# Row maximum of causal attention scores: one reduce over the row, or one per 512-column chunk and a small one over the partial maxima

## The chip, the cores and the metric

The kernel runs on the 8 cores of one Trainium2 chip. Each core works alone on one of the 8 batch entries, with no traffic between cores. The metric is the device time of the slowest core in microseconds.

## What is computed

One transformer block over x of shape (8, 2048, 1024) in float32. The input is normalised (layer norm without weights), and attention and a mixture of experts both read that normalised input; their outputs are added to x. In the reference, cut:

```python
xn = _layernorm(x, axis=-1)
x = x + attn(xn, Wq, Wk, Wv, Wo) + ffn(xn, Wg, W1, W2, W3)
# attn: 16 heads of 64, rotary on q and k
scores = jnp.einsum('bhqd,bhkd->bhqk', q, k) * scale      # T = 2048
scores = jnp.where(causal[None, None], -jnp.inf, scores)
attn = jax.nn.softmax(scores, axis=-1)
out = jnp.einsum('bhqk,bhkd->bhqd', attn, v) ... @ Wo.T
# ffn: 8 experts of hidden size 2730, all computed, weighted by a gate that keeps the top 2
```

## The kernel before

The program is written out by hand, one long list per engine, in the order in which `em(...)` is called. `em` (Builder.emit) is given what each operation reads and writes, as ranges of tiles. It tracks them in slots: 512 columns of the PSUM tile `pp` (one bank), 8 columns of the small statistics tile `stat`, 128 columns of the rest. For each slot it knows the last writer and the readers since, and makes the new operation wait for them on the semaphores of their engines. The writer of a slot also waits for an earlier writer or reader on its own engine, by that engine's own semaphore; a wait that the engine has already made for a later value is left out. Engines run their lists in order.

The stages, in order of time: layer norm of 16 token blocks with the gate and the projections of head pair 0 in between; attention for 8 head pairs, each followed by the projections (L336, with the rotary arithmetic on VectorE) and the V product (L382) of the next pair; the output projection (L533); then the 8 experts (L601, L611, L646), which make up nearly two thirds of the span; the output is transposed and stored at the end.

Attention (`emit_hp_attn`) goes through 32 units for each head pair: 16 query blocks of 128 rows by two heads. Unit qb has L = (qb + 1) * 128 key columns, so 128 to 2048. A unit consists of:

- score matmuls, one for each chunk of up to 512 key columns (L464), each into a PSUM bank of its own. From qb = 8 on every unit uses the same four banks; below, the two heads have two banks each
- the row maximum, negated, over all L columns, on VectorE (L472), into one column of `stat`
- the causal mask, added to the last 128 columns only (L476). The maximum is taken before it: any upper bound of the row will do
- the exponential on ScalarE (L482), with that maximum as bias, which also sums the row; the probabilities go to SBUF in bf16
- then, for the **previous** unit, `s2_stage`: 4 dummy matmuls (L401, whose results nobody reads); transposes of the probabilities in groups of four into banks 4 and 5 in turn, each a matmul by a diagonal matrix of the reciprocal row sums (L416); for each group a copy to SBUF on VectorE (L425); 2 more dummy matmuls; the AV matmuls (L435), which wait for all copies; for the second head a copy of the result on ScalarE (L446)
- last, the reciprocal of this unit's row sum (L491) and the diagonal matrix from it (L494), on VectorE

On VectorE the order in a unit is thus: maximum, mask add, copies of the previous unit, reciprocal, diagonal. On TensorE: scores, four dummies, transposes, two dummies, AV matmuls, scores of the next unit. The statistics of even and odd units stand 16 columns apart in `stat` (`st0`): column 0 has the maximum, 2 the row sum, 5 its reciprocal. Columns 8 to 15 are not used in attention.

Of the kernel before, what the change touches and what calls it, by code (L numbers as in the profile page):

```python
# [10 lines left out]
AX = mybir.AxisListType  # L11
# [125 lines left out]
def build_nc():  # L137
# [20 lines left out]
    with contextlib.ExitStack() as ctx:  # L158
# [14 lines left out]
        stat = en(nc.sbuf_tensor("stat", [128, 64], F32))  # L173
        pp = en(nc.psum_tensor("pp", [128, 4096], F32))
# [8 lines left out]
        em = B.emit  # L183
# [7 lines left out]
        def pps(lo_hi):  # L191
# [4 lines left out]
           writes=[("i128f", 0, 128)], dma="cI128F")  # L196
        em("sync", lambda e: e.dma_start(trineg[:], trineg_in),
           writes=[("trineg", 0, 128)], dma="cTRI")
        em("sync", lambda e: e.dma_start(wgr[:], wg_r),
           writes=[("wgr", 0, 64)], dma="cWGR")  # L200
        em("gpsimd", lambda e: e.dma_start(csb[:, 0:T], ct_in),
           writes=[("csb", 0, T)], dma="cCT")
        em("gpsimd", lambda e: e.dma_start(csb[:, T:2 * T], st_in),
           writes=[("csb", T, 2 * T)], dma="cST")
        em("gpsimd", lambda e: e.dma_start(i128b[:], i128_in),
           writes=[("i128b", 0, 128)], dma="cI128B")
        em("gpsimd", lambda e: e.dma_start(sel8[:], sel8_in),
           writes=[("sel8", 0, 1024)], dma="cSEL")
# [188 lines left out]
        def emit_hp_attn(hp):  # L397
            vb = VH[hp % 2]
            def emit_dummies(n):
                for _ in range(n):  # L400
                    em("tensor", lambda e: e.matmul(  # L401
                        pp[:, 3584:4096], i128b[:], csb[:, 0:512],
                        start=True, stop=True),
                       reads=[("i128b", 0, 128), ("csb", 0, 512)],
                       writes=[("pp", 3584, 4096)])

            def s2_stage(q, a, py):
                prb = PRB if py == 0 else PRB_B
                L = (q + 1) * 128
                ngrp = (q + 4) // 4  # L410
                emit_dummies(4)
                for g in range(ngrp):
                    bank = 4 + (g % 2)
                    kb0 = g * 4
                    kbn = min(4, q + 1 - kb0)
                    em("tensor", [(lambda bk, jj, kk, pr, pyy: lambda e: e.matmul(  # L416
                        pp[:, BK(bk)[0] + jj * 128:BK(bk)[0] + (jj + 1) * 128],
                        pb[:, pr + kk * 128:pr + (kk + 1) * 128],
                        dgb[:, pyy * 128:(pyy + 1) * 128],
                        start=True, stop=True))(bank, j, kb0 + j, prb, py)  # L420
                        for j in range(kbn)],
                       reads=[("pb", prb + kb0 * 128, prb + (kb0 + kbn) * 128),
                              ("dgb", py * 128, (py + 1) * 128)],
                       writes=[("pp",) + BK(bank)])
                    em("vector", (lambda gg, bk, n: lambda e: e.tensor_copy(  # L425
                        pb[:, ATT + gg * 512:ATT + gg * 512 + n * 128],
                        pp[:, BK(bk)[0]:BK(bk)[0] + n * 128]))(g, bank, kbn),
                       reads=[("pp",) + BK(bank)],
                       writes=[("pb", ATT + kb0 * 128, ATT + (kb0 + kbn) * 128)])
                reg = 3072 + (q % 2) * 128  # L430
                emit_dummies(2)
                fns = []
                for kb in range(q + 1):
                    tp = (0, 64) if a == 1 else None
                    fns.append((lambda ax, kk, rr, fi, la, tpp, vbb: lambda e: e.matmul(  # L435
                        pp[64 * ax:64 * ax + 64, rr:rr + 128],
                        pb[:, vbb + kk * 128 + 64 * ax:vbb + kk * 128 + 64 * ax + 64],
                        pb[:, ATT + kk * 128:ATT + (kk + 1) * 128],
                        start=fi, stop=la, tile_position=tpp))(
                            a, kb, reg, kb == 0, kb == q, tp, vb))  # L440
                em("tensor", fns,
                   reads=[("pb", vb, vb + (q + 1) * 128),
                          ("pb", ATT, ATT + L)],
                   writes=[("pp", reg, reg + 128)])
                if a == 1:
                    em("scalar", (lambda hh, qq, rr: lambda e: e.copy(  # L446
                        pb[:, AO + hh * T + qq * 128:AO + hh * T + (qq + 1) * 128],
                        pp[:, rr:rr + 128]))(hp, q, reg),
                       reads=[("pp", reg, reg + 128)],
                       writes=[("pb", AO + hp * T + q * 128, AO + hp * T + (q + 1) * 128)])  # L450

            prev = None
            for qb in range(NB):
                for a in range(2):
                    u = qb * 2 + a
                    py = u % 2
                    st0 = 16 * py
                    prb = PRB if py == 0 else PRB_B
                    L = (qb + 1) * 128
                    nch = (L + 511) // 512  # L460
                    sb0 = 1024 if (a == 1 and qb < 8) else 0
                    for c in range(nch):
                        w = min(512, L - c * 512)
                        em("tensor", (lambda aa, qq, cc, ww, b0: lambda e: e.matmul(  # L464
                            pp[:, b0 + cc * 512:b0 + cc * 512 + ww],
                            pb[64 * aa:64 * aa + 64, QHS + qq * 128:QHS + (qq + 1) * 128],
                            pb[64 * aa:64 * aa + 64, KHS + cc * 512:KHS + cc * 512 + ww],
                            start=True, stop=True))(a, qb, c, w, sb0),
                           reads=[("pb", QHS + qb * 128, QHS + (qb + 1) * 128),
                                  ("pb", KHS + c * 512, KHS + c * 512 + w)],  # L470
                           writes=[("pp", sb0 + c * 512, sb0 + c * 512 + w)])
                    em("vector", (lambda LL, b0, s0: lambda e: e.reduce_max(  # L472
                        stat[:, s0:s0 + 1], pp[:, b0:b0 + LL], axis=AX.X,
                        negate=True))(L, sb0, st0),
                       reads=[("pp", sb0, sb0 + L)], writes=[("stat", st0, st0 + 1)])
                    em("vector", (lambda qq, b0: lambda e: e.tensor_tensor(  # L476
                        pp[:, b0 + qq * 128:b0 + (qq + 1) * 128],
                        pp[:, b0 + qq * 128:b0 + (qq + 1) * 128],
                        trineg[:], ALU.add))(qb, sb0),
                       reads=[("pp", sb0 + qb * 128, sb0 + (qb + 1) * 128), ("trineg", 0, 128)],  # L480
                       writes=[("pp", sb0 + qb * 128, sb0 + (qb + 1) * 128)])
                    em("scalar", (lambda qq, b0, s0, pr: lambda e: e.activation(  # L482
                        pb[:, pr:pr + (qq + 1) * 128], pp[:, b0:b0 + (qq + 1) * 128], AF.Exp,
                        bias=stat[:, s0:s0 + 1], scale=1.0,
                        accum_out=stat[:, s0 + 2:s0 + 3]))(qb, sb0, st0, prb),
                       reads=[("pp", sb0, sb0 + (qb + 1) * 128), ("stat", st0, st0 + 1)],
                       writes=[("pb", prb, prb + (qb + 1) * 128), ("stat", st0 + 2, st0 + 3)])
                    if prev is not None:
                        s2_stage(*prev)
                    prev = (qb, a, py)  # L490
                    em("vector", (lambda s0: lambda e: e.reciprocal(  # L491
                        stat[:, s0 + 5:s0 + 6], stat[:, s0 + 2:s0 + 3]))(st0),
                       reads=[("stat", st0 + 2, st0 + 3)], writes=[("stat", st0 + 5, st0 + 6)])
                    em("vector", (lambda s0, pyy: lambda e: e.tensor_scalar(  # L494
                        dgb[:, pyy * 128:(pyy + 1) * 128], i128b[:],
                        stat[:, s0 + 5:s0 + 6], None, ALU.mult))(st0, py),
                       reads=[("i128b", 0, 128), ("stat", st0 + 5, st0 + 6)],
                       writes=[("dgb", py * 128, (py + 1) * 128)])
            if prev is not None:
                s2_stage(*prev)  # L500
                prev = None
# [7 lines left out]
        for g in range(4):  # L509
# [4 lines left out]
               reads=[("wgate", g * 32, (g + 1) * 32), ("i128f", 0, 128)],  # L514
               writes=[("pp", 3584, 4096)])
            em("vector", (lambda gg: lambda e: e.tensor_copy(
                wrow[0:8, gg * 512:(gg + 1) * 512], pp[0:8, 3584:4096]))(g),
               reads=[("pp", 3584, 4096)], writes=[("wrow", g * 512, (g + 1) * 512)])
# [8 lines left out]
        for mc in range(KC if DO_ATTN else 0):  # L527
            em("gpsimd", (lambda m: lambda e: e.dma_start(
                pbs(WOB[m % 2], 1024), wo_l[m]))(mc),
               writes=[("pb", WOB[mc % 2], WOB[mc % 2] + 1024)], dma="woS")  # L530
            for t in range(NT):
# [7 lines left out]
                   reads=[("pb", WOB[mc % 2], WOB[mc % 2] + 1024)] +  # L539
# [255 lines left out]
```

## Time and profile before

| | us |
|---|---|
| median of 2 runs | 6209.49 (5854.96 and 6564.01) |
| the profiled execution | 5854.8 |
| its span on the slowest core (core 4) | 5852.4 |
| spans of the eight cores in it | 5830.1 to 5852.4 |
| TensorE busy | 5163.3 (88%) |
| VectorE busy | 2469.5 (42%) |
| ScalarE busy | 901.1 (15%) |

The profile is of one execution, on the slowest core. PE is TensorE's matmuls and PEld its weight loads, DVE is VectorE, ACT is ScalarE. PEclk is the share of TensorE's clock that was granted in a stretch: 1.00 is 2.4 GHz and 0.50 is 1.2 GHz. A number such as L472 is a line of the kernel. In the timeline consecutive instructions of one line are merged, with the stretch that they take together.

### The profile page before, as it was taken

Reading aid. Unit: us, or ns where it says so; the run is one execution under the profiler, and the core shown is the slowest. Engines: PE = TensorE matmul, PEld = TensorE weight load, DVE = VectorE, ACT = ScalarE, POOL = GpSimd, SP = SyncE. Lnnn points to the kernel's source line nnn. Section 1 sums busy time; section 2 is a strip of 40 time slices with the busy share of each in tenths; the row PEclk is TensorE's granted clock in tenths of the full one; section 3 lists DMA queues with packets and bytes.
Section 4 is the critical chain, followed back from the end, with each engine's and each line's share of the span. In section 5 each row is a group of like instructions: output and inputs, shape, how many; then the busy total and the mean of one; then the engine's idle time right before and its main releaser. Section 6 shows DMA issues by size and latency. Waiting matters only on the chain.

```text
span 5852.4 us, 74425 instructions; the slowest of 8 cores (5830.1 to 5852.4 us)
## 1 busy us (share of the span) xinstructions
PE 5163.3 (88%) x25926; PEld 2447.8 (42%) x26416; DVE 2469.5 (42%) x4116; ACT 901.1 (15%) x1537; POOL 281.3 (5%) x536
## 2 busy tenths in 40 slices
PE   3357787787788789999999999999999999999998
PEld 2333343334333334444444444444444444444444
DVE  3336656656655523333333333333333333333333
ACT  2222212222222211101101101011011011010110
POOL 0000000000000000000000000000000000000000
PEclk8569989999899989999999999999999999999999
DMA  2010000000000022222222222222222222222222
GB/s 43 18 24 1 10 10 4 7 10 10 1 10 3 4 31 37 44 33 36 41 38 37 40 40 38 37 36 39 38 38 38 39 36 41 42 38 33 37 42 81
DMA packets 81889, 173.86 MB, mean 30 GB/s; under 512 B 9336, under 2 KB 9592, under 8 KB 81536
## 3 DMA queue, kind: packets, MB, share of 16 engines
q0 software_dynamic: 76496, 152.13, 17.3%
q1 hardware_dynamic: 5040, 16.94, 0.8%
q8 instruction: 232, 3.80, 0.3%
q14 instruction: 121, 0.99, 0.1%
HBM read 312.74 MB, written 8.39 MB: 55 GB/s over the span
## 4 chain that ended last, share of the span: by engine, by line
PE 83%; DVE 8%; issue 5%; ACT 2%; DMA 1%; DVEq 0%; ACTq 0%; SPq 0%; POOLq 0%
PE pp L601 21%; PE pp L611 21%; PE pp L646 21%; PE pp L401 5%; PE pp L336 3%; PE pp L435 3%; DVE poolb L425 3%; PE pp L464 3%; DVE stat L472 3%; PE pp L416 1%; PE pp L533 1%; PE pp L382 1%; PE pp L259 1%; ACT poolb L482 1%; PE pp L246 1%
## 5 line engine op out<-in xcount | busy, mean ns | idle before, releaser
L601 PE MATMUL pp<-xn,poolb 128*128 128x512 bf16 x5520 | 1330.7, 381 | 6.2 <-issue 0.4
L611 PE MATMUL pp<-xn,poolb 128*128 128x512 bf16 x5518 | 1324.4, 380 | 6.0
L646 PE MATMUL pp<-poolb 128*128 128x512 bf16 x5518 | 1212.4, 379 | 6.0
L625 DVE TENSOR_TENSOR arf<-pp,arf 128x512 f32<-128x512 f32 x704 | 486.9, 692 | 1442.6 <-PE pp L611 1442.6
L611 PEld LDWEIGHTS pp<-xn,poolb 128*128 128x128 bf16 x5632 | 552.8, 98 | 670.4 <-issue 10.5
L601 PEld LDWEIGHTS pp<-xn,poolb 128*128 128x128 bf16 x5632 | 552.4, 98 | 671.0 <-issue 12.6
L646 PEld LDWEIGHTS pp<-poolb 128*128 128x128 bf16 x5632 | 551.1, 98 | 663.8
L621 ACT ACTIVATE arf<-pp 128x512 f32<-128x512 f32 x704 | 420.3, 597 | 2619.0 <-PE pp L601 2619.0
L401 PE MATMUL pp<-csb,i128b 128*128 128x512 bf16 x1416 | 555.4, 392 | 187.9 <-PE pp L464 31.0
L656 DVE TENSOR_TENSOR acc<-acc,pp 128x512 f32<-128x512 f32 x512 | 352.0, 688 | 845.7 <-PE pp L646 829.6
L631 DVE TENSOR_TENSOR poolb<-arf 128x512 bf16<-128x512 f32 x704 | 487.7, 693 | 74.8 <-DVE arf L625 2.3
L472 DVE TENSOR_REDUCE stat<-pp 128x1 f32<-128x128 f32 (+15 forms) x256 | 330.5, 1291 | 322.2 <-PE pp L464 322.2
L425 DVE CAST poolb<-pp 128x512 bf16<-128x512 f32 (+3 forms) x640 | 364.0, 606 | 156.9 <-PE pp L416 152.8
L482 ACT ACTIVATE poolb<-pp,stat 128x128 bf16<-128x128 f32 (+15 forms) x256 | 298.7, 1167 | 761.0 <-DVE pp L476 595.5
L401 PEld LDWEIGHTS pp<-csb,i128b 128*128 128x128 bf16 x1536 | 148.6, 97 | 545.3 <-issue 539.8
L416 PE MATMUL pp<-dgb,poolb 128*128 128x128 bf16 x2176 | 205.7, 227 | 118.1 <-DVE poolb L425 112.9
L336 PE MATMUL pp<-xn,poolb 128*128 128x512 bf16 x999 | 225.1, 384 | 2.0 <-issue 0.9
L416 PEld LDWEIGHTS pp<-dgb,poolb 128*128 128x128 bf16 x2176 | 145.9, 100 | 174.5 <-issue 152.9
L435 PE MATMUL pp<-poolb 128*64 128x128 bf16 x2176 | 183.6, 235 | 39.8 <-DVE stat L491 32.7
L246 PE MATMUL pp<-i128f,arf 128*128 128x128 f32 x128 | 31.0, 423 | 206.0 <-DVE arf L242 206.0
L435 PEld LDWEIGHTS pp<-poolb 128*64 128x64 bf16 x2176 | 145.7, 119 | 111.1 <-issue 111.1
L593 POOL DMA_DIRECT2D poolb<-w_l x176 | 93.5, 531 | 1975.3 <-PE pp L601 1975.2
(78 smaller groups left out, 1665.6 us busy)
## 6 DMA issues: line engine op xcount, KB each, us to landing
poolb<-w_l POOLq DMA_DIRECT2D x352, 256.0 KB, 4.8
poolb<-w_l POOLq DMA_DIRECT2D x128, 352.0 KB, 4.4
arf<-x SPq DMA_DIRECT2D x16, 512.0 KB, 3.5
out<-arf SPq DMA_DIRECT2D x16, 512.0 KB, 2.8
poolb<-wq_l POOLq DMA_DIRECT2D x8, 256.0 KB, 3.8
poolb<-wqs_l POOLq DMA_DIRECT2D x8, 256.0 KB, 4.7
poolb<-wk_l POOLq DMA_DIRECT2D x8, 256.0 KB, 5.4
poolb<-wks_l POOLq DMA_DIRECT2D x8, 256.0 KB, 5.0
```

The source lines that it names most:

```text
L336: em("tensor", [(lambda bk, wb, kkc, fi, la, a0, a1: lambda e: e.matmul(pps(BK(bk)), pb[:, wb + kkc * 128:wb + (kkc + 1) * 128], xn[:, kkc ...
L401: em("tensor", lambda e: e.matmul(pp[:, 3584:4096], i128b[:], csb[:, 0:512], start=True, stop=True), reads=[("i128b", 0, 128), ("csb", 0, ...
L416: em("tensor", [(lambda bk, jj, kk, pr, pyy: lambda e: e.matmul(pp[:, BK(bk)[0] + jj * 128:BK(bk)[0] + (jj + 1) * 128], pb[:, pr + kk * 12 ...
L425: em("vector", (lambda gg, bk, n: lambda e: e.tensor_copy(pb[:, ATT + gg * 512:ATT + gg * 512 + n * 128], pp[:, BK(bk)[0]:BK(bk)[0] + n * ...
L435: fns.append((lambda ax, kk, rr, fi, la, tpp, vbb: lambda e: e.matmul(pp[64 * ax:64 * ax + 64, rr:rr + 128], pb[:, vbb + kk * 128 + 64 * a ...
L472: em("vector", (lambda LL, b0, s0: lambda e: e.reduce_max(stat[:, s0:s0 + 1], pp[:, b0:b0 + LL], axis=AX.X, negate=True))(L, sb0, st0), re ...
L601: em("tensor", [(lambda cc, tt, bk, kkc, fi, la: lambda e: e.matmul(pps(BK(bk)), pb[:, W1B[cc % 2] + kkc * 128:W1B[cc % 2] + (kkc + 1) * 128],
L611: em("tensor", [(lambda cc, tt, bk, kkc, fi, la: lambda e: e.matmul(pps(BK(bk)), pb[:, W2B[cc % 2] + kkc * 128:W2B[cc % 2] + (kkc + 1) * 128],
L621: em("scalar", (lambda bk, tbb: lambda e: e.activation(arfs(SIL[tbb], 512), pps(BK(bk)), AF.Silu))(b1, tb), reads=[("pp",) + BK(b1)], writ ...
L625: em("vector", (lambda bk, tbb, ebb, tt: lambda e: e.tensor_tensor(arfs(H2S[tbb], 512), pps(BK(bk)), arfs(WBC[ebb] + tt * 512, 512), ALU.m ...
L631: em("vector", (lambda cll, tt, tbb: lambda e: e.tensor_tensor(pb[:, HIDB + cll * T + tt * 512:HIDB + cll * T + (tt + 1) * 512], arfs(SIL[ ...
L646: em("tensor", [(lambda mm, tt, bk, cll, fi, la: lambda e: e.matmul(pps(BK(bk)), pb[:, W3B[mm % 2] + cll * 128:W3B[mm % 2] + (cll + 1) * 128],
```

## The change

For units with more than one chunk of key columns, the one reduce over the row becomes one reduce for each chunk, issued right behind that chunk's score matmul, into columns 8 to 11 of the unit's statistics, and a last reduce over these partial maxima, negated, into the column where the maximum stood. Units with one chunk (L up to 512) keep the one reduce. All else stays, and the exponential reads the same value.

```diff
@@ -469,10 +469,24 @@
                            writes=[("pp", sb0 + c * 512, sb0 + c * 512 + w)])
-                    em("vector", (lambda LL, b0, s0: lambda e: e.reduce_max(
-                        stat[:, s0:s0 + 1], pp[:, b0:b0 + LL], axis=AX.X,
-                        negate=True))(L, sb0, st0),
-                       reads=[("pp", sb0, sb0 + L)], writes=[("stat", st0, st0 + 1)])
+                        if nch > 1:
+                            em("vector", (lambda cc, ww, b0, s0: lambda e: e.reduce_max(
+                                stat[:, s0 + 8 + cc:s0 + 9 + cc],
+                                pp[:, b0 + cc * 512:b0 + cc * 512 + ww],
+                                axis=AX.X))(c, w, sb0, st0),
+                               reads=[("pp", sb0 + c * 512, sb0 + c * 512 + w)],
+                               writes=[("stat", st0 + 8 + c, st0 + 9 + c)])
+                    if nch > 1:
+                        em("vector", (lambda n, s0: lambda e: e.reduce_max(
+                            stat[:, s0:s0 + 1], stat[:, s0 + 8:s0 + 8 + n], axis=AX.X,
+                            negate=True))(nch, st0),
+                           reads=[("stat", st0 + 8, st0 + 8 + nch)],
+                           writes=[("stat", st0, st0 + 1)])
+                    else:
+                        em("vector", (lambda LL, b0, s0: lambda e: e.reduce_max(
+                            stat[:, s0:s0 + 1], pp[:, b0:b0 + LL], axis=AX.X,
+                            negate=True))(L, sb0, st0),
+                           reads=[("pp", sb0, sb0 + L)], writes=[("stat", st0, st0 + 1)])
```

## Rows read from the trace of the kernel before

**Rows 1.** The page: engine busy (share) xinstructions, and the group of the row maximum.
```profile
PE 5163.3 (88%) x25926; PEld 2447.8 (42%) x26416; DVE 2469.5 (42%) x4116; ACT 901.1 (15%) x1537; POOL 281.3 (5%) x536
...
L472 DVE TENSOR_REDUCE stat<-pp 128x1 f32<-128x128 f32 (+15 forms) x256 | 330.5, 1291 | 322.2 <-PE pp L464 322.2
```

**Rows 2.** Windows, attention of pairs 1 to 7: length, busy (x) of PE, PEld, DVE, ACT, POOL.
```profile
586.00:2010.00 1424.00, 1121.19 (x7329) 550.59 (x7452) 857.33 (x1619) 327.58 (x587) 16.36 (x31) 0.95 0.04 7
```

**Rows 3.** Chain of waits, attention stage (411 to 2010 us), shares by line.
```profile
by line: PE pp L401 19.5%; issue 12.3%; PE pp L336 12.1%; PE pp L435 11.2%; DVE poolb L425 10.7%; PE pp L464 10.6%; DVE stat L472 9.9%; PE pp L416 4.9%; PE pp L382 3.2%; ACT poolb L482 2.5%; DVE pp L476 1.4%; DVE stat L491 1.0%; DVEq L691 0
```

**Rows 4.** Timeline, 2048 unit, full clock: start, length, instruction, count, [idle before <-releaser].
```profile
973.90 1.03 PE L464 MATMUL pp<-poolb 64*128 64x512 bf16 x4
...
975.04 2.29 DVE L472 TENSOR_REDUCE stat<-pp 128x1 f32<-128x2048 f32 x1 [1.78 <-PE pp L464]
...
976.67 0.61 PE L416 MATMUL pp<-dgb,poolb 128*128 128x128 bf16 x8
977.43 0.30 DVE L476 TENSOR_TENSOR pp<-pp,trineg_s 128x128 f32<-128x128 f32 x1
977.64 2.48 DVE L425 CAST poolb<-pp 128x512 bf16<-128x512 f32 x4
...
980.26 1.00 PE L435 MATMUL pp<-poolb 128*64 128x128 bf16 x15
...
981.19 1.03 PE L464 MATMUL pp<-poolb 64*128 64x512 bf16 x4
```

**Rows 5.** Timeline, a unit with one chunk (L = 512), full clock.
```profile
848.19 0.39 PE L464 MATMUL pp<-poolb 64*128 64x512 bf16 x1
...
848.68 0.69 DVE L472 TENSOR_REDUCE stat<-pp 128x1 f32<-128x512 f32 x1 [0.48 <-PE pp L464]
```

**Rows 6.** VectorE groups by shape: count, busy us, mean ns, idle before.
```profile
L476 DVE TENSOR_TENSOR pp<-pp,trineg_s 128x128 f32<-128x128 f32 x256 | 76.8, 300 | 27.7 <-DVE stat L472 1.4
...
L472 DVE TENSOR_REDUCE stat<-pp 128x1 f32<-128x2048 f32 x16 | 36.7, 2292 | 44.7 <-PE pp L464 44.7
...
L472 DVE TENSOR_REDUCE stat<-pp 128x1 f32<-128x512 f32 x16 | 11.1, 692 | 7.7 <-PE pp L464 7.7
...
L291 DVE TENSOR_REDUCE stat<-stat 128x1 f32<-128x8 f32 x16 | 2.6, 161 | 1.6
```

**Rows 7.** Timeline of VectorE in the layer norm: a reduce without a wait.
```profile
366.28 1.23 DVE L271 COPY acc<-pp 128x1024 f32<-128x1024 f32 x1 [5.61 <-PE pp L265]
367.42 0.16 DVE L277 TENSOR_REDUCE stat<-pp 128x1 f32<-128x8 f32 x1
```

**Rows 8.** Timeline of VectorE: mask add and first copy at L = 640, at L = 1536.
```profile
860.84 0.30 DVE L476 TENSOR_TENSOR pp<-pp,trineg_s 128x128 f32<-128x128 f32 x1
...
862.05 0.89 DVE L425 CAST poolb<-pp 128x512 bf16<-128x512 f32 x2 [0.91 <-PE pp L416]
...
925.23 0.30 DVE L476 TENSOR_TENSOR pp<-pp,trineg_s 128x128 f32<-128x128 f32 x1
925.49 1.83 DVE L425 CAST poolb<-pp 128x512 bf16<-128x512 f32 x3
```

**Rows 9.** Timeline, 2048 units of pair 1 at half clock (16 such units).
```profile
772.40 2.29 DVE L472 TENSOR_REDUCE stat<-pp 128x1 f32<-128x2048 f32 x1 [3.62 <-PE pp L464]
...
774.83 1.06 PE L416 MATMUL pp<-dgb,poolb 128*128 128x128 bf16 x8
...
775.57 1.29 DVE L425 CAST poolb<-pp 128x512 bf16<-128x512 f32 x2 [0.47 <-PE pp L416]
...
782.31 2.29 DVE L472 TENSOR_REDUCE stat<-pp 128x1 f32<-128x2048 f32 x1 [3.62 <-PE pp L464]
```

**Rows 10.** Windows of head pair 1 and of head pair 2: columns as before, granted clock sixth.
```profile
611.00:799.00 188.00, 146.75 (x937) 71.80 (x951) 108.63 (x211) 46.84 (x84) 1.05 (x2) 0.86 0.04 6
824.00:999.00 175.00, 130.27 (x942) 65.30 (x956) 108.16 (x211) 46.83 (x84) 1.05 (x2) 0.99 0.04 6
```

**Rows 11.** Cores: span and mean granted clock of TensorE.
```profile
core 4: 5852.4 us, clock 0.955
...
core 6: 5831.4 us, clock 0.962
```

## The forecast of the time

> **What bounds the kernel now.** I read the page first. TensorE (PE) is busy for 88% of the span [rows 1]. The table by stage puts attention of head pairs 1 to 7, with the projections between them, into 1424 us [rows 2]. There PE works for 1121 of 1424 us: here the engines wait for each other. The experts' stage behind it is the bulk of the span and does not hold the changed line. The chain of waits over the attention stage [rows 3] gives the changed instruction, the row maximum of L472, 9.9% of 1599 us, that is 158 us. It is busy for 330 us in all [rows 1], so about half of it is covered. Where, and by what, decides the sum.
>
> So I followed one unit (one query block of one head) in the timeline. [rows 4] is a unit with L = 2048 key columns at full clock. Its four score matmuls (L464) start at 973.90. The reduce starts at 975.04, when the last is done, 1.14 us after the first began, and runs 2.29 us. The mask add (L476) starts at 977.43 and the copies of the previous unit (L425) at 977.64. The AV matmuls (L435) wait for the last copy and start at 980.26, and the next unit's score matmuls at 981.19, a period of 7.29 us. PE had the first two groups of transposes (L416) done at about 977.28 (976.67 + 0.61), 0.36 us before the first copy started. So in this unit VectorE (DVE) sets the pace from 975.04 to the end of the copies, and what delays the mask add delays the unit.
>
> It is not so everywhere. With L = 640 [rows 8] the mask add starts at 860.84 and the copy only at 862.05, 1.21 us later, waiting for PE's transposes behind the dummy matmuls. Where nothing else is waited for, that distance is 0.21 us [rows 4], so 1.00 us is cover. At L = 1536 [rows 8] it is 0.26, a cover of 0.05 us. From 1664 columns on I take none, as in [rows 4].
>
> **The change part by part.** Units with L up to 512 (8 of 32 in each of the 8 head pairs) keep their one reduce. In the others (24 of 32) one reduce becomes nch reduces of up to 512 columns, each behind its own score matmul, and one over the nch results. PE, ScalarE (ACT) and the DMA queues issue what they issued before, and no instruction passes another queue's; only DVE's work changes.
>
> Earlier start. With one chunk the reduce starts 0.49 us after its matmul began (848.68 minus 848.19, [rows 5]); with four, 1.14 us [rows 4]. So each full chunk takes 0.217 us of PE time, and the first partial reduce of a 2048 unit starts 0.65 us earlier than the old one. DVE is free then: it had been idle for 1.78 us before 975.04 [rows 4].
>
> More instructions. A reduce takes 692 ns over 512 columns and 2292 ns over 2048 [rows 6]: 1.042 ns a column and 0.159 us fixed. Four of 512 are 2.768 us, 0.48 more. The reduce over the partials I price by L291, the same operation over 8 columns of the same tile: 161 ns [rows 6].
>
> Waits between them. The partial results are columns of one 8-wide tracking slot of stat. So each partial reduce waits on VectorE's own semaphore for the one before it, and the last for all of them. Trace of before: between the old reduce and the mask add, which has such a wait, DVE idles 27.7 us over 256, 0.108 us [rows 6]; I use 0.105 (977.33 to 977.43). There are nch of these waits: nch - 1 between partials, one before the last reduce. The mask add, on the other hand, loses its wait, since the last reduce already waited for everything that it needs. An unheld small reduce behind a long copy starts 0.09 us before that copy's recorded end (367.42 against 366.28 + 1.23, [rows 7]). I take 0.09 of overlap for the mask add; between 0 and that I can't tell, as no unheld instruction behind a tiny reduce stands in the trace.
>
> The Trainium skill ("VectorE: DVE Perf Modes", section "The DRAIN you can't avoid") states that eight copies cost the same with a semaphore after each as with one at the end. This trace disagrees: 0.108 us of idle time with a wait, 0.09 us of overlap without. By that rule the splits would be nearly free; what that would make of the time is rival A.
>
> Sum for a 2048 unit, mask add after the first matmul's start: 0.49 + 2.768 + 4 x 0.105 + 0.161 - 0.09 = 3.75 us. Before: 3.53 us. Later by 0.22 us. For L = 1920 the earlier start is worth 0.05 us less while the fixed terms stay: 0.27; for 1792, 0.32; for 1664, 0.37. For 1536, three chunks: 2 x (0.159 + 0.105) + 0.161 - 0.09 - 2 x 0.217 = 0.165, of which 0.05 is covered: 0.12. For 1408 it is 0.22 against a cover of about 0.19 (my interpolation between 0.05 at 1536 and 1.00 at 640 is 0.14 for each 128 columns): 0.03. Below that the delay (0.14 to 0.36) lies within the cover: nothing. With two units of each length: 2 x (0.22 + 0.27 + 0.32 + 0.37 + 0.12 + 0.03) = 2.66 us a head pair, 21 us over eight.
>
> What hides it at the low clock. Some late units run at half the clock, period 9.91 us instead of 7.29 (772.40 to 782.31, [rows 9]). There the reduce ends at 774.69 and the mask add starts 0.1 later, but the copy starts at 775.57, when the first transposes are done, which began only at 774.83 because of the dummies. PE bounds such a unit; the partial reduces would start still earlier, and the change costs nothing. On the profiled core 16 of the 64 units of 1664 and more columns are of that kind, as the distances between their mask adds in the timeline show. That takes off 16 x 0.3 = 5 us. Direct cost: **+16 us**.
>
> What is late next. ACT's exponential starts after the mask add, on a path of its own that ends before the copies do in the long units; it moves along with them. PE's queue holds transposes 3 and 4, the AV matmuls and the next scores behind the copies: its quiet stretch, from 977.28 to 980.26 in [rows 4] 3.0 us with 8 transposes and 2 dummies in it, grows by the 0.2 to 0.4 us. The clock fell only in units with 1792 columns and more, where that stretch is longest, and oftenest in the 2048 ones. In [rows 10] the head pair with five units at half clock takes 188 us in the window where one with none takes 175. The eight cores of this one execution differ by 21 us with the granted clock, 0.955 to 0.962 [rows 11]. A stretch 0.3 us longer puts a unit where one with some 256 columns more stood. I estimate about one more unit at half clock in each head pair, at 1.2 to 2.6 us (the low period against the full one, whole or in part): **+12 us**, half of what separates the cores. The lower bound of this term is 0, the upper is rival B.
>
> The Trainium skill ("TensorE: Matmul & The Clock Gate", section "HAM oscillation — how this bites in real kernels") says that a kernel whose matmul groups are parted by long waits falls back to the low clock again and again. It speaks against this change, and the trace agrees as far as the last units of [rows 9] go.
>
> 5855 + 16 + 12 = 5883 us. The profiled execution took 5854.8 us by the clock of the run, 5852.4 its span, and the sum stands against that; the median of the two runs shown (6209.49) lies 6% higher, halfway between 5854.96 and 6564.01, and my number is for an execution like the profiled one and the lower of the two.
>
> **The rivals.**
> A, the split is free or gains. If the waits between dependent reduces cost nothing and they overlap by 0.09 us, the mask add of a 2048 unit comes at 0.49 + 2.768 - 4 x 0.09 + 0.161 - 0.09 = 2.97 us, 0.56 earlier. The copies then wait for PE's transposes and only 0.32 us of it counts (the 0.36 us above less 0.04 to 0.05 from a group's end to its copy); for 1920 about 0.18, for 1792 0.05, less below: 1.1 us a head pair, -9 us, 5846 us. With waits of zero and no overlap the delays are between 0 and 0.05 us: 5855. Against it: [rows 6] show 0.108 us behind exactly this kind of instruction. A variant of it: the delay is real, but PE covers more than I read. Together 5840 to 5862.
>
> B, the low clock takes over (slower than before). If PE's longer quiet stretch brings each head pair to five low units as pair 1 has [rows 10], the cost is 13 us a pair, 104 us, of which the profiled execution already pays about 39 (the 16 units): +65 us, and about 5 to 10 for the delay in the rest: 5925 us. From 2% on (5972 us) about 60 low units at 2.6 us would be needed instead of 16, 7 to 8 in every pair: all from 1664 columns on. For it: the stretch grows in just these units. Against it: pair 2 had not one in this execution [rows 10], and 0.3 us is a tenth of the stretch.
>
> C, DVE pays more than I took. If the mask add does not overlap but waits as before, each unit is 0.2 us later: 2 x 6 x 0.2 x 8 = 19 us more, 5900 us. The two ends of that price (-0.09 and +0.105) bound it.
>
> **How the numbers follow.** The forecast, 5865 to 5905 with C in it, 0.6. A, 0.15. B short of 2%, 5905 to 5970, 0.2; B beyond 2%, 0.04. Something that I don't see, such as fewer falls of the clock by luck, 0.01. The predicted time is the forecast's, 5883. The range takes in A's lower bound and most of B: 5845 to 5930. Differences within 2% (117 us) are about what a measurement of this kernel can't tell from no change: same 0.94; slower 0.05, B in full; faster 0.01, as nothing on the path shortens by so much.
>
> **What would show it.** In the profile after: the partial reduces over 512 columns at 692 ns, with idle time of about 0.105 us between them; the small reduce at about 160 ns; the mask add of a 2048 unit 3.75 us after its first score matmul; a period of 7.5 us at full clock, unchanged for L up to 1280. Right in the total by accident if the periods stay and the clock alone changes. Wrong, if the partial reduces follow without a gap (A), or if the windows of the head pairs all show a clock under 0.9 (B).

## The result, and the profile after

The changed kernel takes 5923.88 us in the median of 11 runs (from 5904.09), the kernel before 5877.14 us in the median of 10 (from 5854.96). The ratio is 1.0088, 95% interval [1.0066, 1.0110]: about 52 us slower, within the 2% band. In some executions of every kernel the four cores of one die show a lower clock and take some per cent longer; the ratios, and the means over cores further down, leave these out, which is why the medians differ by less. The profiled execution took 5902.4 us, 47.6 more than the one profiled before.

The page and the table of cores after: VectorE's reduces are 576 instead of 192 in the units with more than one chunk (beside 192 small ones), and the clock is lower on every core (before: 0.955 to 0.962). TensorE's busy time can't be compared from the two pages: the trace of core 4 lacks 490 matmul records that this one, of core 0, has. On one and the same core it rises by 25 us (core 3) to 61 us (core 1), on core 4 by 37 us (5163.3 to 5200.4).

```profile
PE 5264.9 (89%) x26416; PEld 2466.2 (42%) x26416; DVE 2544.5 (43%) x4692; ACT 901.6 (15%) x1537; POOL 282.4 (5%) x536
...
L473 DVE TENSOR_REDUCE stat<-pp 128x1 f32<-128x512 f32 (+3 forms) x576 | 360.0, 625 | 221.6 <-PE pp L464 181.3
```

```profile
core 0: 5900.0 us, clock 0.946
...
core 5: 5870.8 us, clock 0.955
```

The groups by shape, count, busy us, mean ns, idle before (answering to [rows 6]). The partial reduces cost what a reduce of 512 cost before, the small one 157 ns, and the mask add (L490) has lost its idle time: 7.5 us over 256 where it was 27.7.

```profile
L473 DVE TENSOR_REDUCE stat<-pp 128x1 f32<-128x512 f32 x432 | 298.8, 692 | 206.3 <-PE pp L464 181.3 <-PE pp L416 0.5
L490 DVE TENSOR_TENSOR pp<-pp,trineg_s 128x128 f32<-128x128 f32 x256 | 74.8, 292 | 7.5 <-issue 0.5 <-DVE stat L486 0.5
...
L480 DVE TENSOR_REDUCE stat<-stat 128x1 f32<-128x4 f32 x64 | 10.0, 157 | 7.6 <-DVE stat L473 1.1
```

The timeline of a unit with L = 1920 at full clock, core 0, from its score matmuls to those of the next unit (it answers to [rows 4], with 128 columns less):

```profile
1810.11 0.98 PE L464 MATMUL pp<-poolb 64*128 64x512 bf16 x4
1810.60 2.94 DVE L473 TENSOR_REDUCE stat<-pp 128x1 f32<-128x512 f32 x4 [1.08 <-PE pp L464]
...
1812.83 0.61 PE L416 MATMUL pp<-dgb,poolb 128*128 128x128 bf16 x8
1813.65 0.16 DVE L480 TENSOR_REDUCE stat<-stat 128x1 f32<-128x4 f32 x1
1813.72 0.29 DVE L490 TENSOR_TENSOR pp<-pp,trineg_s 128x128 f32<-128x128 f32 x1
1813.92 2.34 DVE L425 CAST poolb<-pp 128x512 bf16<-128x512 f32 x4
...
1817.28 0.98 PE L464 MATMUL pp<-poolb 64*128 64x512 bf16 x4
```

The first partial reduce starts 0.49 us after the first score matmul, as worked out. Four of them take 2.94 us with three waits of about 0.1 us in between (2.634 for the reduces alone). The mask add comes at 3.61 us; the forecast sum for 1920 columns was 3.62. Before, it came at 3.35. The period is 7.17 us. With 2048 columns the mask add comes at 3.75 us, the forecast's number (median in e5, described below; before 3.54).

From the traces of all eight cores I took the distance from one unit's first score matmul to the next one's, where the clock was full throughout (median; of 1920 and 2048 columns the first or second unit of the two, as given), and the time at half clock between the first score matmul and the start of the last unit:

| | before | after | later | forecast |
|---|---|---|---|---|
| L up to 1280 | 3.33 to 5.40 us | the same | 0.00 | 0 |
| L = 1408 | 5.450 | 5.465 | 0.015 | 0.03 |
| L = 1536 | 5.728 | 5.822 | 0.094 | 0.12 |
| L = 1664 | 6.101 | 6.463 | 0.362 | 0.37 |
| L = 1792 | 6.541 | 6.850 | 0.309 | 0.32 |
| L = 1920, first | 6.917 | 7.173 | 0.256 | 0.27 |
| L = 2048, first | 7.293 | 7.50 (in e5, where the clock stays full; pairs 0, 1, 3) | 0.21 | 0.22 |
| attention, mean of the cores | 1575.7 us | 1623.6 us | 47.9 | 28 |
| of it at half clock | 118 us | 229 us | 111 | |

One thing in these periods was not in the sum. In the second unit with L = 1664 and in the first with 2048, VectorE has in most pairs one gap that is longer than elsewhere, and the period is up to 0.35 us longer for it. It stands at another instruction from pair to pair. On core 7 of e5 a partial or the small reduce waits 0.46 us instead of 0.105, or the mask add or the first copy starts 0.23 or 0.13 us behind the instruction ahead of it instead of 0.08 or 0.09 us before its end; pairs 6 and 7 have none with 1664 columns, pairs 0, 1 and 3 none with 2048. The gaps of 0.46 us stand in the same pair at the same instruction on all eight cores. The second 1664 unit of pair 2 on core 7:

```profile
927.06 2.68 DVE L479 TENSOR_REDUCE stat<-pp 128x1 f32<-128x512 f32 x4 [0.86 <-PE pp L470]
...
930.19 0.16 DVE L486 TENSOR_REDUCE stat<-stat 128x1 f32<-128x4 f32 x1 [0.46 <-DVE stat L479]
```

In two such units, a packet of the instruction queue q14 (8 KB) started within the unit, 3.9 to 4.3 us after its first score matmul and in both 0.6 us behind the end of the gap. Such a packet starts in these two units in all eight pairs of this core, 3.1 to 4.8 us after the first score matmul, also in the pairs without a longer gap. VectorE's list is longer now and q14 carries 131 packets, before 121. That the gap has to do with the fetch of instructions is a guess from this and not shown. At up to 0.35 us, twice a pair, it is at most 6 us.

All of the loss is in attention: what lies outside it takes 4259 to 4269 us a core before and 4259 to 4266 after.

### The profile page after: what moved, and what is told of

It reads as the page before. It is cut to its first block, busy times and chain, and to the rows that moved or that the text cites. A ratio compares the mean times of both kernels' runs of the same rounds, so it can differ in the third digit from the quotient of the medians.

```text
span 5900.0 us, 76259 instructions; the slowest of 8 cores (5870.8 to 5900.0 us)
## 1 busy us (share of the span) xinstructions
PE 5264.9 (89%) x26416; PEld 2466.2 (42%) x26416; DVE 2544.5 (43%) x4692; ACT 901.6 (15%) x1537; POOL 282.4 (5%) x536
## 4 chain that ended last, share of the span: by engine, by line
PE 83%; DVE 9%; issue 5%; ACT 2%; DMA 1%; DVEq 0%; ACTq 0%; SPq 0%; POOLq 0%
PE pp L615 21%; PE pp L625 21%; PE pp L660 20%; PE pp L401 6%; PE pp L336 3%; PE pp L435 3%; DVE poolb L425 3%; DVE stat L473 3%; PE pp L464 2%; PE pp L416 1%; PE pp L547 1%; PE pp L382 1%; PE pp L259 1%; PE pp L246 1%; PE pp L265 0%
## 5 line engine op out<-in xcount | busy, mean ns | idle before, releaser
L401 PE MATMUL pp<-csb,i128b 128*128 128x512 bf16 x1536 | 618.5, 403 | 153.6
L473 DVE TENSOR_REDUCE stat<-pp 128x1 f32<-128x512 f32 (+3 forms) x576 | 360.0, 625 | 221.6 <-PE pp L464 181.3
```

The costliest lines, as they stand in the source:

```text
L401: em("tensor", lambda e: e.matmul(pp[:, 3584:4096], i128b[:], csb[:, 0:512], start=True, stop=True), reads=[("i128b", 0, 128), ("csb", 0, ...
L473: em("vector", (lambda cc, ww, b0, s0: lambda e: e.reduce_max(stat[:, s0 + 8 + cc:s0 + 9 + cc], pp[:, b0 + cc * 512:b0 + cc * 512 + ww], a ...
```

## The experiments

For each run the ratio to the kernel before stands with its 95% interval. "Attention" is the mean over the cores of the profiled execution, "half clock" the part of it at a granted clock of 0.50.

| | ratio | attention, us | half clock, us |
|---|---|---|---|
| before | 1 | 1575.7 | 118 |
| the change | 1.0088 [1.0066, 1.0110] | 1623.6 | 229 |
| e1: before, mask add delayed | 1.0132 [1.0089, 1.0174] | 1639.9 (cores 0 to 3) | 291 (cores 0 to 3) |
| e2: the change for L to 1536 only | 1.0032 [1.0011, 1.0052] | 1601.2 | 196 |
| e8: e2 again | 1.0046 [1.0020, 1.0072] | 1591.4 | 161 |
| e3: partials don't wait for each other | 0.9922 [0.9896, 0.9949] | 1530.8 | 17 |
| e4: before, with dummies | 0.9952 [0.9932, 0.9973] | 1550.0 | 26 |
| e5: the change, with dummies | 0.9994 [0.9978, 1.0010] | 1565.5 | 5 |
| e6: e3 with dummies | 0.9924 [0.9899, 0.9949] | 1528.6 | 8 |
| e7: before, one unit a pair delayed | none (one execution counts) | 1580.4 | 125 |
| e9: before, two units a pair delayed | 1.0008 [0.9935, 1.0081] | 1595.6 | 182 |
| e10: e2 with dummies | 0.9981 [0.9962, 1.0000] | 1563.9 | 63 |

The theory, called D below: the split delays the mask add and the copies behind it; this costs the time directly in the long units, and once more because TensorE's longer quiet stretch makes its clock fall more often. The rival, S: something of the split itself, its many semaphores and small reads of PSUM, disturbs TensorE.

**e1: the delay without the split.** In the kernel before, in units with four chunks, behind the one reduce:

```diff
+                    if nch == 4:
+                        for j in range(2):
+                            em("vector", (lambda jj, s0: lambda e: e.reduce_max(
+                                stat[:, s0 + 8:s0 + 9],
+                                stat[:, s0 + (8 if jj else 0):s0 + (9 if jj else 1)],
+                                axis=AX.X))(j, st0),
+                               reads=[("stat", st0 + (8 if j else 0), st0 + (9 if j else 1))],
+                               writes=[("stat", st0 + 8, st0 + 9)])
```

> The kernel before with its one reduce, and behind it, in the units with four chunks (L from 1664), two tiny reduces on VectorE that depend on each other. They do nothing but delay the mask add: by 2 x (0.105 + 0.161) + 0.071 - 0.266 = 0.34 us a unit, about what the changed kernel does to these units (0.36 to 0.21). Theory D (the delay of the mask add and nothing else of the split costs the time, half of it directly and half through TensorE's clock): direct 8 x 8 x 0.34 = 22 us less what falls in units at half clock, about 18, and 25 to 35 us more by the clock; ratio 1.007 to 1.010, time at half clock per core in attention up from 118 us to over 200. Rival S (the many semaphores or small reads of PSUM of the split themselves disturb PE's clock): 18 to 22 us alone, ratio 1.003 to 1.004, and half-clock time as before.

Measured: ratio 1.0132. The tiny reduces show up as worked out, 154 ns each:

```profile
L479 DVE TENSOR_REDUCE stat<-stat 128x1 f32<-128x1 f32 x128 | 19.7, 154 | 14.0 <-DVE stat L473 0.5 <-DVE stat L479 0.5
```

The full-clock periods are 0.32 to 0.33 us longer in these units (6.43, 6.86, 7.24 us against 6.10, 6.54, 6.92), 21 us over the 64 of them. On cores 0 to 3, the ones that count here, attention takes 62 us more than on the same cores before, and 291 us of it are at half clock instead of 124. No split is needed for either part of the loss: S falls as the explanation of the changed kernel (e3, further down, has the change's partial reduces and next to no half-clock time, which speaks against S too). The ratio is above the 1.007 to 1.010 that theory D gave. The clock's part is larger than I expected, and larger than with the change, whose delay is smaller in just the longest units (0.21 to 0.26 us against 0.32), where the clock falls most. Not all of it lies in the long units: 31 of the 291 us are in the first 24 units of the pairs, where the kernel before has none and e1 delays nothing (more on such falls under e10).

**e2 and e8: the split in the short units alone.** `if nch > 1` became `if 1 < nch < 4` in both places, so that units from L = 1664 keep the one reduce.

> The change in the units with two and three chunks alone (L 640 to 1536); from 1664 on the one reduce stays. Theory D: these units have cover, direct cost 2 x (0.10 + 0.02) x 8 = 2 us, and their clock never falls, so the time is that of before within 3 us, ratio 1.000, and half-clock time about 118 us a core. Rival S: the clock falls here too, +10 us and more.

> The kernel of e2 once more (the split in the units with two and three chunks alone), to see whether its surplus repeats: e2 gave 1.003 and 196 us a core at half clock where e7, with a like delay made otherwise, gave 125. Both theories on e2 expect 1.002 to 1.004; if it was the luck of that chip or hour, 1.000.

Measured: 1.0032 and 1.0046, not 1.000. The periods behave as in the table above (5.822 us at 1536, 6.104 at 1664), the direct cost is the 2 us expected, and still half-clock time goes up to 196 and 161 us. Of these, 35 and 21 us lie in the first 24 units of the pairs, where the kernel before has none, and 86 us in both runs in the last unit and the projections behind it (before 61). The full-clock periods in these two places are those of before, but for the 0.02 to 0.09 us at 1408 and 1536 columns. That was a miss: a surplus of 10 us and more was what rival S expected of e2. e7, e9 and e10 were made for it.

**e3: partial maxima that don't wait for each other.** The changed kernel, with the partial results in slots of their own (in a wider stat), read with a stride by the last reduce:

```diff
-                                stat[:, s0 + 8 + cc:s0 + 9 + cc],
+                                stat[:, 64 + 2 * s0 + 8 * cc:65 + 2 * s0 + 8 * cc],
...
-                            stat[:, s0:s0 + 1], stat[:, s0 + 8:s0 + 8 + n], axis=AX.X,
+                            stat[:, s0:s0 + 1],
+                            stat[:, 64 + 2 * s0:96 + 2 * s0].rearrange(
+                                "p (c w) -> p c w", w=8)[:, 0:n, 0:1], axis=AX.XY,
```

> The changed kernel with each partial maximum in a tracking slot of its own (8 columns apart, read with a stride by the last reduce), so that the partial reduces do not wait for each other. Forecast from the rows: gaps between partials go from +0.105 us to between -0.04 and -0.09; the mask add of a 2048 unit comes 3.16 us after its first score matmul (before 3.53, changed 3.75), where the copies then wait for TensorE's transposes. Periods at full clock against the kernel before: -0.31 (2048), -0.18 (1920), -0.05 (1792), 0 (1664 and below): -9 us in all. With the clock falling less often than before: 10 us more. Theory D: 5830 to 5850 us, ratio 0.995 to 0.999. If the wait on the own semaphore costs nothing beyond what the engine needs anyway: the same as the changed kernel, ratio 1.009.

Measured: ratio 0.9922, 46 us faster than before and faster than the forecast for it. Timeline of a 2048 unit at full clock (core 3):

```profile
955.70 1.03 PE L464 MATMUL pp<-poolb 64*128 64x512 bf16 x4
...
956.19 2.48 DVE L473 TENSOR_REDUCE stat<-pp 128x1 f32<-128x512 f32 x4 [0.80 <-PE pp L464]
...
958.47 0.61 PE L416 MATMUL pp<-dgb,poolb 128*128 128x128 bf16 x8
958.79 0.16 DVE L480 TENSOR_REDUCE stat<-stat 128x1 f32<-128x4 f32 x1
958.86 0.29 DVE L492 TENSOR_TENSOR pp<-pp,trineg_s 128x128 f32<-128x128 f32 x1
959.06 2.61 DVE L425 CAST poolb<-pp 128x512 bf16<-128x512 f32 x4
```

Four partial reduces of 512 columns take 2.48 us in all, less than 4 times 0.692: each starts 0.09 us before the recorded end of the one ahead. In the changed kernel the same four take 3.075 us (2.768 and three gaps; median over its 2048 units). The wait on the engine's own semaphore is worth 0.2 us a time, gap and lost overlap together. The mask add comes 3.16 us after the first score matmul, as forecast. The copies start 0.20 us later, at 3.36 us and not at the 3.43 that I had for the transposes' end: the first copy waits for the first group of four transposes alone (done at about 958.85), not for both groups. So the periods fall by more than worked out: 6.906 us at 2048 (by 0.39), 6.585 at 1920 (0.33), 6.335 at 1792 (0.21), 6.029 at 1664 (0.07), which is 16 us over the eight pairs. The clock gives most of the rest: 17 us at half clock instead of 118, worth 26 us at the price worked out under e5. Together 42 of the 45 us by which attention is shorter.

**e4, e5, e6: keeping the clock up.** Three dummy matmuls before the third group of transposes, in units whose previous query block has 13 or more key blocks; in the kernel before (e4), the changed one (e5) and e3's (e6):

```diff
+                    if g == 2 and q >= 12:
+                        em("tensor", [lambda e: e.matmul(
+                            pp[:, 3584:4096], i128b[:], csb[:, 0:512],
+                            start=True, stop=True)] * 3,
+                           reads=[("i128b", 0, 128), ("csb", 0, 512)],
+                           writes=[("pp", 3584, 4096)])
```

> The kernel before with three more dummy matmuls (0.82 us at full clock) in the stretch of 1.2 us in which TensorE waits for the first copy, ahead of the third group of transposes, in units whose previous query block has 13 or more key blocks. If the clock falls because TensorE has too little to do in this stretch, half-clock time goes from 118 us a core to under 40, which at 0.27 us for each us of it (from the two traces: 31 us over 111) gives -20 to -30 us: ratio 0.995 to 0.997. If the clock doesn't depend on that stretch: no less half-clock time, and the dummies cost up to 0.3 us in each unit at half clock: 1.000 to 1.002.

> The changed kernel with the same three dummy matmuls in TensorE's wait for the first copy, in the late units. With the clock kept up, what is left of the change is its direct cost. Theory D: periods at full clock of the changed kernel stay (6.46, 6.85, 7.17, 7.50 us for L 1664, 1792, 1920, 2048), half-clock time per core in attention falls from 229 us to under 60, and the time lies 18 to 22 us above e4 (the kernel before with these dummies), that is ratio 0.998 to 0.999 to the kernel before. If the splits disturb the clock by themselves, half-clock time stays above 120 us and the ratio above 1.002.

> Partial maxima in slots of their own (e3) and the dummies (e4) together. In e3 only 17 us a core were left at half clock, so the dummies have at most 4 us to give back, and could cost as much where they delay the third group of transposes, which now is waited for earlier. Forecast: same as e3 within 4 us, ratio 0.991 to 0.993. If the gains of e3 and e4 were independent: 0.987.

Measured: 0.9952, 0.9994, 0.9924. Timeline in e4 (L = 1920, core 7): the dummies (L415) lie in the stretch in which TensorE waited for the first copy, and the third group of transposes still starts when the copy lets it, 1.03 us after the mask add's start, as before (977.43 to 978.47 in the 2048 unit of [rows 4] was 1.04). First the line of that third group in the kernel before, with TensorE's wait of 1.19 us ahead of it, then e4:

```profile
978.47 0.39 PE L416 MATMUL pp<-dgb,poolb 128*128 128x128 bf16 x4 [1.19 <-DVE poolb L425]
```

```profile
1976.46 0.61 PE L422 MATMUL pp<-dgb,poolb 128*128 128x128 bf16 x8
1976.90 0.81 PE L415 MATMUL pp<-csb,i128b 128*128 128x512 bf16 x3
1977.09 0.30 DVE L482 TENSOR_TENSOR pp<-pp,trineg_s 128x128 f32<-128x128 f32 x1
1977.30 2.47 DVE L431 CAST poolb<-pp 128x512 bf16<-128x512 f32 x4
...
1978.12 0.38 PE L422 MATMUL pp<-dgb,poolb 128*128 128x128 bf16 x4 [0.41 <-DVE poolb L431]
```

The dummies are not free everywhere: the second 1664 unit and the first 1792 unit, the first two that have them, are 0.06 us longer than before (6.41 and 6.60 us). From the second 1792 unit on the periods are those of before. Half-clock time in the units from 1664 columns on goes from 58 us to 2, and in the last unit and the projections behind it from 61 us to 0; the 26 us that are left lie in the first 24 units, on three cores. In e5 attention runs at full clock on core 7 but for 10 us (length, busy of PE, PEld, DVE, ACT and POOL, granted clock):

```profile
412.00:1982.00 1570.00, 1271.14 (x8457) 600.10 (x8454) 1032.18 (x2394) 371.28 (x667) 16.88 (x32) 1.00 0.04 6
```

This splits the cost of the change. With the dummies in both, e5 stands 15.5 us above e4 in attention and e4 still has 22 us more at half clock, worth 6 us: the direct cost is 21 us at full clock, as forecast. (The ratio of e5 itself, 0.9994, lies just above the expected 0.998 to 0.999, which its interval holds; by the ratios it stands 25 us above e4.) And the dummies take 58.1 us off the changed kernel by removing 225 us at half clock: 0.26 us for each us of it. Single units give the same price: with 1920 columns a unit wholly at half clock takes 9.59 us in both kernels, against 6.92 us at full clock before and 7.17 us after, that is 0.28 and 0.25 us for each us. The 111 us that the change adds to half-clock time are then 29 us, which with 19 us of direct cost (21 less what falls on units at half clock) makes the 48 measured. In e6 next to nothing was left to win, as expected, and the ratio is e3's.

**e7, e9, e10: the surplus of e2.** e7 has e1's two tiny reduces in one unit of each pair alone (`if qb == 11 and a == 0`). e9 has one reduce over 90 columns in each of the two units with L = 1536, dependent on the maximum:

```diff
+                    if qb == 11:
+                        em("vector", (lambda s0: lambda e: e.reduce_max(
+                            stat[:, s0 + 8:s0 + 9], trineg[:, 0:90], axis=AX.X))(st0),
+                           reads=[("stat", st0, st0 + 1), ("trineg", 0, 128)],
+                           writes=[("stat", st0 + 8, st0 + 9)])
```

e10 is e2 with the dummies.

> The kernel before with a delay of 0.34 us (two tiny dependent reduces on VectorE) in one unit of each head pair alone, with L = 1536: 0.29 us beyond its cover, 2.3 us in all. e2 had about the same delay in sum (0.22 us a pair, before the long units) and yet 15 us more in the mean over the cores, with 196 us at half clock instead of 118, all of it in units that it doesn't change. Theory P (the late units meet a fall of the clock or not by when they start, and any small shift ahead of them moves that): half-clock time differs from 118 us here too, by 30 us or more, in the late units, and the time by 8 us or more beyond the 2.3. Theory S (what counts in e2 is the splits): half-clock time of 100 to 140 us, ratio 1.000 to 1.001.

> The kernel before, with one small dependent reduce over 90 columns on VectorE in the two units with L = 1536, sized to make these units longer by 0.095 us each, as the split does in e2 (5.822 against 5.728 us), with no split anywhere. Theory P (only when the late units start counts): as e2, ratio 1.002 to 1.004, half-clock time 170 to 220 us a core. Theory S (the splits count): 1.000 to 1.001, half-clock time 100 to 140 us.

> The kernel of e2 with the three dummy matmuls of e4 in the late units. If the surplus of e2 is the clock alone, it goes: 2 us above e4, ratio 0.995 to 0.996, half-clock time under 40 us a core. If it is something else, e4 + 15 us: 0.998.

Measured: e7 has 125 us at half clock, like before, in the one execution that counts (5853.6 us): no surplus, as theory S had it. e9, whose two units came out at 5.825 us (the 5.822 of e2), has 182 us at half clock in its profiled execution, as theory P had it. But the mean span of the eight cores is 5860 us in that execution and 5844 to 5847 us in its three others that count, where the kernel before has 5833 to 5855 us in 21 of 22. In e2 and e8 it is 5851 to 5866 us in all 13. So the surplus comes back each time in e2 and was seen once in e9, whose ratio, 1.0008 with 0.7% to both sides, decides nothing. e10 missed its forecast too (0.9981 and 63 us at half clock; 0.995 to 0.996 and under 40 were expected). It has no half-clock time left behind unit 16 of the pairs; the 63 us lie at their beginnings. Core 5, windows from the start of pair 3 and of pair 2 over their first eight units:

```profile
1011.00:1045.00 34.00, 29.20 (x86) 8.40 (x83) 12.05 (x39) 6.33 (x20) 0.53 (x1) 0.56 0.06 8
812.00:837.00 25.00, 20.34 (x91) 7.13 (x88) 12.05 (x39) 6.33 (x20) 0.53 (x1) 1.00 0.07 11
```

The same VectorE work (12.05 us, 39 instructions) takes 34 us at clock 0.56 and 25 at 1.00. So the clock costs time in short units too, which is not where theory D has it. Between e10 and e4 lie 14 us of attention; 37 us more at half clock (10 us) and the 2 us of direct cost make most of it.

These falls (stretches of up to 10 us aside) are of two kinds. One begins in the third unit of a pair (L = 256), whose work no kernel here changed; e10 has it in pair 3 on seven of eight cores, and e2, e3, e4, e6, e8 and e9 have it on one to four cores. The other begins in the 17th or 18th unit (L = 1152), in e1, e2, e4, e8 and, in pair 7 on five cores, in e9. e4 and e9 have no split, so a split is not needed for either kind. The kernel before shows neither, and the changed kernel has only 2 us a core at half clock in its first 24 units, so they are no part of its loss. What brings them about is open. A shift of when a pair begins is what e2, e9 and e10 have in common, but e7 has one as well and shows next to none (1 us a core). That the split in the short units makes them more frequent is not excluded, as e2 and e8 show a surplus each time.

## Why the prediction was off by half

The range, 5845 to 5930, held the median, 5923.88 us, and a difference within 2% is what came. The predicted time, 5883, and the band that I gave the forecast, up to 5905, did not: the result lies in the band of rival B short of 2%, which had 0.2. (The profiled execution, 5902.4 us, is still inside the forecast's band; it was the fastest of the changed kernel.) Over its profiled predecessor the change was forecast at 28 us and cost 48.

*What bounds a unit, and where.* Right. The periods did not change up to 1280 columns, and from 1664 on the whole delay shows in them.

*The direct sum.* Right to 0.03 us in every length of the table, 2.5 us a pair against 2.66; the longer gaps in two units of most pairs were not foreseen. The earlier start (0.49 us), the price of a short reduce, the 0.105 us waits and the overlap of 0.09 us at the mask add are all in the timeline after. Direct cost 19 us, forecast 16. (By the same terms the delays below 1408 columns are 0.12 to 0.33 us, not the 0.14 to 0.36 of the text; within the cover either way.)

*Units at half clock cost nothing more.* Consistent: a first 2048 unit wholly at half clock takes 9.91 us in the median both before and after, and a 1920 unit 9.59 us. One such 2048 unit of the changed kernel, window, core 0 (the granted clock, 0.50, is third from the end):

```profile
1825.20:1835.10 9.90, 8.77 (x41) 4.10 (x40) 5.90 (x12) 2.06 (x2) 0.00 (x0) 0.50 0.00 1
```

*The clock term.* This step failed. I forecast one more unit at half clock in each pair, at 1.5 us, 12 us in all. The runs show 29 us: the change puts 111 us more of attention at half clock, and each of them costs 0.26 us. At that price the forecast's 12 us are 46 us at half clock, so the term was 2.4 times too small. How much of that is the number of units and how much their price depends on how they are counted. Units from 1664 columns on that spend over half of their period at half clock, without the last unit of a pair, went from 4.5 to 14.3 a core, 1.2 more a pair, which makes the number about right and the price 3.0 us instead of 1.5. Counted as the forecast did, by the distance between mask adds and with the last unit, they went from 10.9 to about 22, 1.4 more a pair at 2.6 us. Either way the price was the larger error. One such unit more comes with 10 to 11 us more at half clock, since nearly each fall also takes part of the unit ahead or behind, or of the projections: I had priced the unit as a mean over whole and partial ones, when the partial ones come on top. The 16 units of the forecast were those of core 4, which has the most half-clock time of the eight, 167 us against a mean of 118. The span of the cores in one execution, which I used as a second measure, says nothing on the mean.

*Rival A.* Its mechanism, reduces that follow each other without a gap, does not hold for the change, as I had argued from the idle time in [rows 6]. The rule of the Trainium skill that was weighed there, "VectorE: DVE Perf Modes", section "The DRAIN you can't avoid", that a semaphore after each operation costs nothing extra, disagrees with these runs: with the waits four reduces take 3.075 us, without them (e3) 2.48. But I undersized the gain: the cover by the transposes was read to the end of both groups, and the first copy needs one. With 2.48 us, a 2048 unit gains 0.39 us and not the 0.32 I allowed as the most. (The text also says that the range takes in A's lower bound; that is 5840, and the range begins at 5845.)

*Rival B.* This is what the result turned out to be in size, by the mechanism named for it: in the late units the quiet stretch of TensorE grows by 0.2 to 0.36 us, and the clock falls more often. e1 shows it with the delay alone and e5 by taking the falls away. The sign that I had named for it, windows of all pairs under a clock of 0.9, did not come: those of pairs 1 and 2 on core 0 show 0.92 and 0.93. The Trainium skill ("TensorE: Matmul & The Clock Gate", section "HAM oscillation — how this bites in real kernels") has matmul groups parted by long waits fall back to the low clock; the traces agree, and here the longest wait within the quiet stretch is 1.2 us (977.28 to 978.47 in the unit of [rows 4]). e4 shows that even the kernel before paid for it: 26 us less in attention with three dummies a unit.

*Rival C.* Excluded: the mask add overlaps (it starts at 1813.72 us, 0.09 us before the small reduce's end).

## What to carry to other kernels

Splitting an operation to start it earlier pays only when what is gained at the start is more than the fixed cost and the wait of every piece. Look at what the dependency tracking will make of the pieces' results: four results in one tracked slot turned a gain of 46 us into a loss of 52 us, with the same arithmetic. Where TensorE has little to do in a stretch, price a delay twice: once directly, and once for the clock, with the time at half clock read from the trace and not the count of slow units. Here a few dummy matmuls in a wait that is there anyway told the two apart.

## What I had not expected of the hardware

- A wait on VectorE's own semaphore between two reduces over 512 columns costs 0.2 us: a gap of 0.105 us instead of an overlap of 0.09 us.
- Three dummy matmuls, 0.81 us together, in a wait of 1.2 us, brought the time at half clock in the late units from 58 us to 2 a core.
- The clock can also fall in the short units of a head pair: single stretches of 34 to 79 us at half clock that begin in the third unit, of 3.3 us at full clock, whose work no kernel here changed.
- VectorE has single longer gaps in two units of most pairs, up to 0.46 us between dependent instructions where the others are 0.105 us, at another instruction from pair to pair.
